# Starting the MLP's first quarter inside the attention's last two iterations, in a one-core AdaLN block with a learned rotation

## The reference, cut to what matters

```
ada = silu(c) @ W_ada + b_ada                  # shift, scale and gate, for attention and for MLP
h   = layernorm(x) * (1 + scale_msa) + shift_msa
x   = x + gate_msa * (attention(h) @ W_proj + b_proj)          # 16 heads of 9 channels
h   = layernorm(x) * (1 + scale_mlp) + shift_mlp
x   = x + gate_mlp * (gelu(h @ W_fc1 + b_fc1) @ W_fc2 + b_fc2) # 576 hidden channels
U   = Q factor of qr(P)                        # P is 144 x 64
R   = expm(skew matrix from silu(c) @ W.T + b) # one 64 x 64 matrix per batch
out = x + ((x @ U) @ R - x @ U) @ U.T
```

## Time and profile before

| | |
|---|---|
| median of 3 runs | 316.73 us (315.64 to 318.06) |
| the profiled execution's own time | 316.29 us |
| its span on the core | 314.5 us (1.79 us lie around the span) |
| mean granted PE clock | 0.962 |
| PE / DVE / ACT / POOL busy | 276.2 / 212.9 / 130.2 / 103.4 us |
| chain that ended last, by engine | PE 71%, DVE 18%, issue 6%, ACT 3% |

### The profile page before, as it was taken

How to read it: one execution, slowest core, us unless ns; L and a number is a source line. 1 busy time by engine, 2 the same in 40 slices (tenths; PEclk the granted TensorE clock), 3 DMA queues, 4 the chain that set the end, 5 groups by cost and what they waited for, 6 DMA issues and landing times.

```text
span 314.5 us, 8835 instructions
## 1 busy us (share of the span) xinstructions
PE 276.2 (88%) x3215; PEld 200.4 (64%) x3215; DVE 212.9 (68%) x948; ACT 130.2 (41%) x274; POOL 103.4 (33%) x298
## 2 busy tenths in 40 slices
PE   2897889789899979899999898999886599999995
PEld 1756355576676667776776677677664434765983
DVE  6128573878888887899978756766677465832543
ACT  2123314455464535455644545544544235350321
POOL 7412231433422623345343223322233286400000
PEclk9999969999999988999999979999999679999999
DMA  7928000000000000000000000000000000000013
GB/s 214 248 56 300 4 7 4 9 11 10 4 2 2 0 3 2 2 3 1 5 2 1 2 2 2 3 2 3 2 3 2 0 2 0 4 0 2 0 40 113
DMA packets 9779, 8.44 MB, mean 27 GB/s; under 512 B 2064, under 2 KB 9334, under 8 KB 9608
## 3 DMA queue, kind: packets, MB, share of 16 engines
q1 hardware_dynamic: 9380, 7.11, 7.9%
q10 hardware_dynamic: 356, 0.75, 0.8%
HBM read 6.40 MB, written 1.20 MB: 24 GB/s over the span
## 4 chain that ended last, share of the span: by engine, by line
PE 71%; DVE 18%; issue 6%; ACT 3%; ACTq 1%; POOL 0%; DVEq 0%
PE banks L1369 6%; PE banks L1443 6%; PE banks L1601 5%; PE banks L1338 5%; PE banks L1333 5%; PE banks L1585 4%; PE banks L1381 4%; PE banks L1201 4%; PE banks L1334 4%; PE banks L1397 4%; PE banks L1447 3%; DVE qstk L969 2%; PE banks L1418 2%; DVE cB L914 2%; PE banks L1407 2%
## 5 line engine op out<-in xcount | busy, mean ns | idle before, releaser
L412 POOL TENSOR_TENSOR root<-rec,mhalf 128x1 f32<-128x1 f32 x63 | 34.4, 545 | 140.6 <-DVE Z L910 140.4
L969 DVE TENSOR_REDUCE qstk<-banks 128x8 f32<-128x1024 f32 x32 | 39.0, 1218 | 5.0 <-PE banks L1369 4.8
L895 DVE RECIPROCAL rec<-banks 128x1 f32<-128x1 f32 x63 | 10.3, 163 | 37.9 <-PE banks L1447 34.5
L551 ACT ACTIVATE E<-banks 128x1024 f32<-128x1024 f32 x32 | 32.8, 1025 | 7.0 <-PE banks L1381 6.8
L1443 PE MATMUL banks<-Z,ident 128*128 128x65 f32 x126 | 26.0, 289 | 10.1 <-DVE Z L916 9.6
L1443 PEld LDWEIGHTS banks<-Z,ident 128*128 128x128 f32 x126 | 19.5, 194 | 19.2 <-issue 11.1
L1381 PEld LDWEIGHTS banks<-QM,KT 32*128 32x128 f32 x512 | 17.5, 187 | 14.4 <-issue 14.4
L1369 PE MATMUL banks<-KT,QT 32*128 32x128 f32 x512 | 24.7, 310 | 1.7 <-DVE wskT L714 1.6
L1381 PE MATMUL banks<-QM,KT 32*128 32x128 f32 x512 | 23.4, 297 | 1.2 <-issue 1.2
L1369 PEld LDWEIGHTS banks<-KT,QT 32*128 32x128 f32 x512 | 18.5, 197 | 8.4 <-issue 8.3
L1447 PE MATMUL banks<-Z,ident 128*128 128x64 f32 (+62 forms) x126 | 22.9, 262 | 0.4 <-DVE Z L916 0.4
(11 more groups left out here) (249 smaller groups left out, 624.1 us busy)
## 6 DMA issues: line engine op xcount, KB each, us to landing
gates<-gates_dram SPq DMA_DIRECT2D x1, 2304.0 KB, 10.2
x_all<-in_x_dram SPq DMA_DIRECT2D x4, 288.0 KB, 6.2
out_dram<-x_all SPq DMA_DIRECT2D x8, 144.0 KB, 2.0
wskew<-in_L_cond_W_dram SPq DMA_DIRECT2D x4, 283.5 KB
A<-v SPq DMA_DIRECT2D x63, 4.0 KB
wada<-in_L_cond_W_ada_dram ACTq DMA_DIRECT2D x1, 432.0 KB
wfc1a<-in_L_cond_W_fc_dram SPq DMA_DIRECT2D x1, 288.0 KB
wfc2a<-in_L_cond_W_fc_dram SPq DMA_DIRECT2D x1, 288.0 KB
```

What stands on the lines that cost most here:

```text
L412: link(nc.gpsimd.tensor_tensor(root[:, at], rec[:, at], mhalf[:, 0:1], ALU.pow))
L551: nc.scalar.activation(E[:, g, :, :, :].rearrange("p r j t -> p r (j t)"), scored(g), ACT.Exp).then_inc(s_E, 1)
L969: nc.vector.tensor_reduce(qstk[b % 2][:, 8 * g:8 * g + 8, D:D + 1].rearrange("p (j r) a -> p r (j a)", r=4), scored(g).rearrange("p r (j m ...
```

## The change

The first quarter's batches are normalized at the end of iteration 14 on DVE instead of at the end of 16. PE transposes their four 128-channel parts in one block into bank 4 at the end of iteration 15, DVE (not ACT) modulates them; then PE transposes the four rests in one block into the same bank in iteration 16 and DVE modulates those. Each block is one wait and one signal, so `m_xnT` counts 2 where it counted 4 for the four batches. U's three parts move behind these blocks, and `scaled_UT` moves behind `gated(14)`. The flag loads stand at the end of iteration 16, and on PE the load waits for `UT`. `products` and the first two `fc1_main` are placed between the steps that close batch 15, `M_all` is copied by ACT instead of DVE, and `fc1_last` and `fc1_rest` of the first quarter follow between the transposes of batches 4 to 7. From the second quarter on the code is as it was.

```diff
@@ ACT @@
+            def products_copied():
+                act.wait_ge(s_Mp, 1)
+                for n in range(4):
+                    nc.scalar.activation(M_all[:, 2 * n:2 * n + 2, :].rearrange("p s c -> p (s c)"), bank[n][:, 0:2 * C],
+                                         ACT.Copy).then_inc(s_M, 1)
+
             def attention(b):
                 if weighing(b):
                     exponentials(b - 1, 0)
                 if only(b, B + 1):
-                    modulated_main(0)
-                    modulated_main(1)
+                    products_copied()
...
-                if only(b, B + 1):
-                    modulated_main(2)
-                    modulated_main(3)
...
                         modulated_main(4 * Q + 4 + j)
-                    if j == 0:
+                    if j == (1 if Q == 0 else 0):
                         gelu(Q, FK)
@@ DVE @@
+            def first_modulated_main():
+                dve.wait_ge(m_xnT, 1)
+                for b in range(4):
+                    cols = slice(128 * b, 128 * b + 128)
+                    TS(hT1q[0][:, cols], bank[4][:, cols], mod1[:, 3, b:b + 1], mod1[:, 2, b:b + 1],
+                       ALU.mult, ALU.add).then_inc(m_hT, 1)
+            def first_modulated_rest():
+                dve.wait_ge(s_mod2r, 2)
+                dve.wait_ge(m_xnT, 2)
+                for b in range(4):
+                    cols = slice(128 * b, 128 * b + 128)
+                    TS(hT2q[0][:, cols], bank[4][:, cols], mod2r[:, 1, b:b + 1], mod2r[:, 0, b:b + 1],
+                       ALU.mult, ALU.add).then_inc(m_h2, 1)
...
+                    if q == 0 and b == B:
+                        first_modulated_main()
                     if q == 1 and within(b, 3, B + 1):
                         statistics(b - 3)
                     if q == 1 and b == B + 1:
-                        modulated_rest(0)
+                        U_copied()
                     if q == 1 and closing(b):
                         divided(b - 2)
-                    if q == 1 and b == B + 1:
-                        modulated_rest(1)
+                    if q == 1 and b == B:
+                        first_modulated_rest()
+                        transposed_E()
+                        normalized_again(4)
+                        normalized_again(5)
+                    if q == 2 and b == B + 1:
+                        normalized_again(6)
...
-                    if q == 0 and b == B:
-                        transposed_E()
-                    if q == 1 and b == B:
-                        scaled_UT()
-                    if q == 3 and b == B:
-                        U_copied()
-                        dve.wait_ge(s_mod2r, 2)
+                    if q == 3 and b == B - 2:
                         for j in range(4):
                             normalized_again(j)
-                    if q == 2 and b == B + 1:
+                    if q == 3 and b == B:
+                        scaled_UT()
                         more_squarings_then_R()
+                    if q == 3 and b == B + 1:
+                        normalized_again(7)
+                        modulated_rest(4)
+                        modulated_rest(5)
+                        statistics(B - 1)
@@ PE @@
+            def first_main_T():
+                pe.wait_ge(m_xn, 8)
+                pe.wait_ge(s_Y, 1 + SQ)
+                for b in range(4):
+                    ins = pe.transpose(bank[4][:, 128 * b:128 * b + 128], xnq[:, b, :], ident[:, :])
+                ins.then_inc(m_xnT, 1)
+            def first_rest_T():
+                pe.wait_ge(m_hT, 4)
+                for b in range(4):
+                    ins = pe.transpose(bank[4][:, 128 * b:128 * b + 128], xrq[:, b, :, :].rearrange("p a n -> p (a n)"), ident[:, :])
+                ins.then_inc(m_xnT, 1)
...
             def more_squarings():
-                pe.wait_ge(s_E, 2 * B)
-                pe.wait_ge(s_oT, 2 * B)
+                pe.wait_ge(s_UT, 2)
+                pe.wait_ge(s_oT, 2 * B - 2)
                 asked = pe.value_load(flag[0:1, 0:1])
...
                 if b == B + 1:
-                    transposed_again(0)
+                    products()
...
                 step(b, 1, heads_back if closing(b) else None)
                 if b == B + 1:
-                    transposed_again(1)
+                    pe.wait_ge(s_ldm, 16 * (7 + 2 * FK))
+                    fc1_main(0, 0)
...
                 if b == B:
-                    U_parts(b, 0)
+                    first_rest_T()
...
                 if b == B:
-                    U_parts(b, 1)
+                    U_parts(b, 0)
                 step(b, 2)
...
                 if b == B + 1:
-                    more_squarings()
-                    transposed_again(2)
+                    fc1_main(0, 1)
...
+                if b == B:
+                    U_parts(b, 1)
                 step(b, 3, projection if closing(b) else None)
-                if b == B + 1:
-                    transposed_again(3)
+                if b == B:
+                    more_squarings()
+                    U_parts(b, 2)
...
+                if b == B - 1:
+                    first_main_T()
...
+            fc1_main(0, 2)
+            transposed_again(4)
+            fc1_main(0, 3)
+            transposed_again(5)
+            fc1_last(0)
+            transposed_again(6)
+            fc1_rest(0)
+            transposed_again(7)
+            for Q in range(1, NQ):
```

More of the change, by code:

```diff
@@ L512, in modulated_main @@
             def modulated_main(b):
-                act.wait_ge(m_xnT, b + 1)
+                act.wait_ge(m_xnT, b - 1)
                 wait(act, m_fc1, b // 4 - 1)
-                nc.scalar.activation(hT1q[b // 4 % 2][:, 128 * (b % 4):128 * (b % 4) + 128], main_bank(b)[:, 0:128], ACT.Identity,
+                nc.scalar.activation(hT1q[b // 4 % 2][:, 128 * (b % 4):128 * (b % 4) + 128], bank[7][:, 0:128], ACT.Identity,
                                      bias=mod1[:, 2, b:b + 1], scale=mod1[:, 3, b:b + 1]).then_inc(m_hT, 1)
@@ L869, in normalized_again @@
             def normalized_again(b):
-                wait(dve, m_xnT, b - 3)
+                if b >= 4:
+                    dve.wait_ge(m_xnT, max(2, b - 5))
                 dve.wait_ge(s_rstd2, b // 4 + 1)
@@ L944, in transposed_E @@
             def transposed_E():
+                dve.wait_ge(s_diag, 2)
+                nc.vector.tensor_reduce(usc[:, 0:1], dG[:, :], AX.X, ALU.add).then_inc(s_dred, 1)
+                nc.vector.tensor_reduce(usc[:, 1:2], dB[:, :], AX.X, ALU.add).then_inc(s_dred, 1)
                 dve.wait_ge(s_ETp, 1)
@@ L1070, in _ @@
                 attention(b)
[L1072 to L1077, removed]
             def x2_made(b):
@@ L1097, in rotated_added @@
                     TT(two, two, bank[3 + n][:, 0:2 * C], ALU.add).then_inc(m_out, 1)
-            products_evacuated()
             for Q in range(NQ):
[L1101 to L1104, removed]
+                if 1 <= Q < NQ - 1:
                     for j in range(4):
@@ L1325, in transposed_again @@
                 wait(pe, m_h2, b)
+                if b == 4:
+                    pe.wait_ge(s_on, B)
+                    pe.wait_ge(s_pr, B)
                 if b >= 12:
                     pe.wait_ge(m_tmp, b // 4 * 4 - 8)
-                pe.transpose(main_bank(b)[:, 0:128], xnq[:, b % 4, :], ident[:, :])
-                pe.transpose(rest_bank(b)[:, 0:128], xrq[:, b % 4, :, :].rearrange("p a n -> p (a n)"), ident[:, :]).then_inc(m_xnT, 1)
+                pe.transpose(bank[7][:, 0:128], xnq[:, b % 4, :], ident[:, :])
+                pe.transpose(bank[6][:, 0:128], xrq[:, b % 4, :, :].rearrange("p a n -> p (a n)"), ident[:, :]).then_inc(m_xnT, 1)
             def qkv(b):
@@ L1553, in _ @@
             generator_weights(3)
-            for b in range(0, B + 2):
-                attention(b)
             def products():
                 pe.wait_ge(s_R, 1)
-                pe.wait_ge(s_pr, B)
-                pe.wait_ge(m_hT, 4)
-                pe.wait_ge(m_h2, 4)
+                pe.wait_ge(s_UT, 2)
+                pe.wait_ge(s_E, 2 * B)
                 for c in range(NC):
@@ L1574, in fc1_last @@
                 wait(pe, m_gT, 5 * Q - 4)
+                if Q == 0:
+                    pe.wait_ge(s_U, 5)
                 for n in range(2):
@@ L1603, in fc2 @@
                 mm(dst, gTl[Q % 2][:, 128 * (b % 2):128 * (b % 2) + 128], wfc2b[:, n, :], start=False, stop=True).then_inc(m_fc2, 1)
+            for b in range(0, B + 2):
+                attention(b)
             def x2_T(Q):
@@ L1636, in rotated @@
                 ins.then_inc(m_rot, 1)
-            pe.wait_ge(s_ldm, 16 * (7 + 2 * FK))
-            pe.wait_ge(s_U, 5)
-            for Q in range(NQ):
-                if Q == 0:
-                    products()
+            fc1_main(0, 2)
[7 more added lines that the diff above has]
+            for Q in range(1, NQ):
                 fc1_last(Q)
                 for k in range(FK):
```

(2 more changed lines are left out.)

24 lines of the change are left out of this document (7 added, 17 removed).

## The result

The changed kernel takes 313.14 us (median of 21 runs, 311.97 to 317.96), the kernel before, run beside it on the same chip, 317.99 (21 runs, 314.19 to 321.56): a ratio of 0.9891 with a 95% interval of 0.9864 to 0.9918, so about 1.1% less. Its profiled execution took 312.01 us, against a forecast of 311.6.

The account below looks back on a forecast made before the run. PE, without a stop from the second quarter on, bounds the kernel, so that quarter's first product sets the time. 314.5 - 6.75 (order less shift) + 2.1 (clock) + 1.79 = 311.6 us, range 309.0 to 315.5.

Parts of the forecast that it names:

- The bound: PE never stops from the MLP's second quarter on; the question is how much earlier than 261.79 us its first product starts.
- The shift by DVE: Iteration 14: eight normalizations ahead of the row maximum make it 1.14 us late, on the path; cost taken as 1.15 us.
- Iteration 15 "nothing": Iteration 15 on PE: four transposes, some 0.5 us, cost nothing as long as DVE's gate is the later one.
- The order, 7.9 us: Iterations 16 and 17: reordering starts the second quarter at 253.9 instead of 261.79, 7.9 us earlier, 6.75 less the shift.
- The clock: At the flag PE has nothing from 240.8 to 242.75, so a clock fall is likelier than not; price 2.1 us.
- The sign given for the fall: First "fc1_main" about 3.6 us behind the start of U's transposes if the clock falls, 2.6 if not.
- Sum: Whole kernel: 314.5 - 6.75 + 2.1 = 309.85, plus 1.79 around the span, gives 311.6 us.
- Late next is ACT's table load: First quarter's end: ACT's 1.28 us table load, between modulations of batches 5 and 6, is what is late next.
- No fall at the flag: Rival: the clock stays full at the flag, 309.5 us; chance 0.20.
- Two falls: Rival: the clock also falls in iteration 15, a short spell doubling about 1.5 us: 313.1, up to 315 us; chance 0.24.
- The order yields less: Rival: eight modulations and PE-DVE hand-overs take longer, "UT" 1.5 us later: 313.1 us, or 314.5; chance 0.10.
- Slower: Rival: clock falls at the flag and stays at 1.2 GHz until the second quarter: 318.5 us; chance 0.06.

Follow-up runs that it names:

- e8: The kernel before with only the normalizations of batches 0 to 3 moved to iteration 14, all else in old order: median 316.68 us, ratio 0.999.
- e11: The kernel before with eight one-column DVE instructions added in iteration 1, their result unread: 321.87 us in one run.
- e12: The changed kernel with eight one-column DVE instructions added in iteration 1, their result unread: 313.23 us in one run.
- e2: The changed kernel with 16 identity transposes, read by nobody, ahead of PE's flag load: median 313.35 us, no ratio worked out.
- e3: The changed kernel with PE's flag load moved to iteration 14, the branch left in place: median 314.99 us, ratio 0.9838.
- e6: The kernel before with 12, 14 and 14 unread identity transposes in three PE waits of iteration 17: median 314.97 us, ratio 0.994.
- e4: The changed kernel with a one-element gelu on ACT at the end of iteration 16, loading its table early: median 314.41 us, ratio 0.9914.
- e1: The changed kernel with three of the four early normalizations in an earlier DVE hole of iteration 14: median 313.77 us, ratio 0.9872.
- e5: The changed kernel with unread identity transposes, 10 ahead of iteration 15's weighing scores and 16 ahead of the flag load: median 310.23 us, ratio 0.9689.
- e7: The changed kernel with three normalizations earlier, flag load in iteration 14, early gelu table and 12 identity transposes ending iteration 16: median 309.61 us, ratio 0.9738.
- e10: Same edits as e7, plus the first quarter's fc1_rest in two halves with batch 7's transposes between: median 308.89 us, ratio 0.9756.

## Why the prediction was right, step by step

**The bound.** Right: PE's stream from the second quarter on was untouched, 30.00 of 30 us busy and 52.8 us long, and the time followed that quarter's first product.

**The shift by DVE.** Forecast 1.14 us, measured 1.03 (2.32 less 1.29). The eight normalizations take 224.65 less 222.56, 2.09 us, with POOL's one addition beside them, against 1.92 in quiet: 0.17 for the addition, 0.2 forecast. Only the one "xrq" that runs beside it is longer, 0.48 us against 0.30. The Trainium skill, page "SBUF — State Buffer", section "Who interferes with whom", has whoever issues first hold the shared port pair for its whole instruction while the other fully blocks. The prediction took from this that the addition's whole 0.49 us would go, and that did not happen. The rows do not speak against the Trainium skill, though: the "xrq" ends at 223.29, 0.05 us behind the addition's end (222.72 and 0.52), as if it had waited for it, and loses only 0.18: the rest of the addition ran beside the "xnq" ahead and in the 0.30 us that the "xrq" takes anyway. How long it was blocked, no row shows.

**Iteration 15 "nothing".** The four transposes cost nothing: "15" is 11.35 us with them and in e8 without them. The step still failed by 0.35 us, which the prediction put at nothing: DVE's gate, the later one there as it assumed, itself came 0.35 us later, for the place in DVE's program (e8, e11, e12). No row of before could have told.

**The order, 7.9 us.** Measured 7.67: from batch 14's second values to the product 27.06 us before, 19.39 in e2 at full clock. The row of before at which this begins:

```profile
234.66 0.64 PE L1397 MATMUL banks<-E,V 128*32 128x128 f32 x16 [0.68 <-DVE tmp L922]
```

The pieces hold too. With 1.34 us of shift taken off, the second modulations end at 238.33 (forecast 238.3), the gate is at 240.98 (240.7), "UTr" ends at 241.81 (241.65), U's transposes start at 242.91 (242.75). The e2 trace, shifted likewise, has the first main product at 245.63 (245.3) and the second quarter at 254.05 (253.9).

**The clock.** Forecast that it falls at the flag, at 2.1 us; it does, at 1.98. That the price fits is luck in part: it was the middle of 1.25 for a short spell and 2.95 for a long one. The low spell lasts some 6.8 us (242.6 to 249.4), the long one of the earlier trace rows, but it starts 1.6 us ahead of U's transposes, while PE has nothing to do, and so cost less than 2.95. The short spell of e3 cost 1.24 by the estimate there, near the 1.25. The sign given for the fall shows the same: the first main product starts 4.23 us behind U's transposes (244.25 to 248.48), where 3.6 was named, and 2.67 in e2 without the fall (2.6). Of the 7.67 us of "order", at least 2.24 were the price of the old fall (e6), which the prediction does not set apart; with 1.98 paid again, the change won little by the clock.

**Sum.** Forecast for the stretch +1.15 - 7.9 + 2.1 = -4.65; measured +1.03 + 0.35 - 7.67 + 1.98 = -4.31. So 0.34 of the 0.4 us by which the profiled execution missed its forecast lie in this stretch, and the 0.35 of iteration 15 are as large.

**"Late next is ACT's table load."** Half wrong: it is on the chain, but taking it away wins 0.24 us (e4), since batch 7's hand-over from PE to ACT and back ends 0.24 us earlier and no more.

**The rivals.** "No fall at the flag" is what the transposes bring about; the plain order fell in every profile that kept it (changed, e1, e3, e4, e12). "Two falls" is real, at its forecast price of 1.5 us, in some executions: of six profiles with the idle of 1.28 us (changed, e2, e3, e4, e8, e12) two fell in iteration 15, and of seven without it (before, e1, e5, e6, e7, e10, e11) none. How often it does so in the 21 runs stays open. The median, 1.1 us above the profiled execution, does not show it: the median run has a mean granted clock of 0.966, the profiled one 0.967, so about as much low time in all. Only six of the 21 have a lower one (0.951 to 0.961), and they took 314.0 to 317.96 us. Four took 314.81 to 316.14 at 0.966 or 0.967, and why stays open. Some of the scatter may be the loop ahead: in the eleven programs without the eight small instructions, the gate of iteration 14 came at 222.26 to 231.52 us, in work that the edits all but leave alone; the low slices of their rows of granted clock lie at different places of the loop. "The order yields less" put "UT" 1.5 us later; "UTr" ended 0.16 later than forecast. "Slower" had its price from a spell of 17 us; it was 6.8.

## What to carry to other kernels

Give a sum its terms by stretches between two fixed instructions, and compare variants by the same stretches: here the whole times of one kernel scatter by 6 us, while a piece without a fall agreed to 0.03 us in the eight programs that have the later DVE step ("15", 11.34 to 11.37). Filling a chain's holes with other work moved the bound here by what the single file of waits allowed; what remained was hand-overs between engines and the clock that fell in the last hole, and sixteen transposes that nobody reads were worth 2 us there (e2). A fall's price hangs on what PE has to do while the clock is low, not on the length of the spell alone. Before splitting a group of small matmuls, see whether they run side by side.

## What the runs showed of the hardware that was not expected

- The place of an instruction in an engine's program can cost time: the same DVE step took 0.36 us more with eight instructions more ahead of it, and not with sixteen more (e8, e11, e12).
- Four products of 17 rows in four bands of the array take 1.14 us, two of them 1.13 (e10).
- On PE a flag's load and branch took 1.10 us from the end of what they waited for to the next matmul; with the load moved ahead 0.55 were left (e3).
- The clock fell behind an idle of 1.28 us in some executions of the same order and not in others, and ten transposes in that hole left it at full clock in the one profile taken (it fell in e2 and e3, not in the changed kernel, e4 and e12; e5).
- Low spells at the same flag lasted 6.8 us in the changed kernel and 3.4 in e3, and cost 1.98 and, by an estimate, 1.24 us.
